# A Mamba block with butterfly FFN on one core: three moves in VectorE's order of work

## What is computed

```python
x = x + ssm(layernorm(x));  x = x + ffn(layernorm(x))
# ssm: xz = x @ in_proj_w.T; x_inner, z = split(xz)            (512 channels each)
#      x_conv = silu(causal_conv_4_taps(x_inner) + conv_b)
#      delta, B, C = split(x_conv @ x_proj_w.T), delta = softplus(delta)   (16 states)
#      h = h * exp(delta * A) + x_conv * (delta * B);  y = h . C           (scan over tokens)
#      return ((y + x_conv * D) * silu(z)) @ out_proj_w.T
# ffn: h = butterfly(x @ W_exp + b_exp); h = gelu(h + up_bias); h = butterfly(h)
#      return h @ W_con + b_con + down_bias
```

## Time and profile before

| | us |
|---|---|
| median of 3 runs | 543.41 (543.35 to 543.48) |
| the profiled execution | 543.8 |
| its span in the trace | 542.1 |
| PE busy in it | 516.0 (95%) |
| DVE busy in it | 416.8 (77%) |
| ACT busy in it | 307.0 (57%) |
| mean granted clock of PE | 0.981 of full |

### The profile page before, as it was taken

How to read it: one execution, slowest core, us unless ns; L and a number is a source line. 1 busy time by engine, 2 the same in 40 slices (tenths; PEclk the granted TensorE clock), 3 DMA queues, 4 the chain that set the end, 5 groups by cost and what they waited for, 6 DMA issues and landing times.

```text
span 542.1 us, 8227 instructions
## 1 busy us (share of the span) xinstructions
PE 516.0 (95%) x3012; PEld 422.5 (78%) x3012; DVE 416.8 (77%) x892; ACT 307.0 (57%) x537; POOL 93.3 (17%) x88
## 2 busy tenths in 40 slices
PE   4989999998999999999999999999999999889997
PEld 3756776776887788878888788888888789578886
DVE  4778999888984999489975999489956986576542
ACT  2777883794249622875269722964278514951242
POOL 4040200220211202140211211030213021122020
PEclk9995988999999999999999999999999999999999
DMA  9652511200112001210112002110021001200011
GB/s 223 134 28 3 83 39 41 66 16 2 39 40 76 6 2 50 69 41 1 40 40 81 0 2 79 54 28 2 0 79 42 1 1 39 81 0 1 1 40 39
DMA packets 42635, 21.75 MB, mean 40 GB/s; under 512 B 26435, under 2 KB 41027, under 8 KB 42596
## 3 DMA queue, kind: packets, MB, share of 16 engines
q1 hardware_dynamic: 39956, 17.57, 13.9%
q10 hardware_dynamic: 2640, 3.67, 2.4%
HBM read 16.78 MB, written 4.46 MB: 39 GB/s over the span
## 4 chain that ended last, share of the span: by engine, by line
PE 58%; DVE 20%; ACT 9%; issue 9%; POOL 2%; DMA 1%; DVEq 0%; ACTq 0%; POOLq 0%
PE wide L715 11%; PE acc L877 11%; PE wide L866 9%; PE wide L855 9%; DVE xc L1516 5%; PE wide L829 4%; DVE state L1621 3%; PE small L705 3%; PE wide L840 2%; ACT xc L1186 2%; DVE diag_sum L1639 2%; DVE diag L1635 2%; DVE hid_low L1533 1%; PE wide L725 1%; PE small L735 1%
## 5 line engine op out<-in xcount | busy, mean ns | idle before, releaser
L1146 ACT ACTIVATE hid_f<-wide,bias_up 128x512 f32<-128x512 f32 x64 | 43.9, 686 | 160.5 <-PE wide L866 157.5
L1516 DVE SCALAR_TENSOR_TENSOR xc<-xi,taps,xc 128x512 f32<-128x512 f32 x96 | 96.2, 1007 | 4.5 <-ACT xc L1177 2.3
L877 PE MATMUL acc<-w_down_high,hid_high 128*128 128x256 f32 x256 | 73.7, 288 | 3.5 <-DVE hid_low L1533 3.4
L877 PE MATMUL acc<-w_down_high,hid_low 128*128 128x256 f32 x256 | 72.0, 281 | 0.0
L877 PE MATMUL acc<-w_down_low,hid_high 128*128 128x256 f32 x256 | 72.0, 281 | 0.0
L1533 DVE TENSOR_TENSOR hid_low<-hid_f,hid_high 128x512 fp32r<-128x512 f32 x64 | 47.4, 743 | 15.5 <-ACT hid_high L1259 15.2
L855 PE MATMUL wide<-w_out,xc 128*128 128x256 f32 x256 | 58.4, 388 | 0.7 <-DVE xc L1660 0.5
L715 PE MATMUL wide<-xnT_ln1T_high,w_in_high 128*128 128x512 f32 x128 | 56.7, 443 | 0.0
L877 PEld LDWEIGHTS acc<-w_down_high,hid_high 128*128 128x128 f32 x256 | 48.3, 188 | 10.2 <-issue 6.6
L866 PE MATMUL wide<-xnT_ln2T_high,w_up_high 128*128 128x512 f32 x128 | 54.2, 424 | 1.7 <-DVE xnT_ln2T_low L1527 1.7
L855 PEld LDWEIGHTS wide<-w_out,xc 128*128 128x128 f32 x256 | 49.2, 194 | 7.8 <-issue 1.1
(11 more groups left out here) (193 smaller groups left out, 1035.3 us busy)
## 6 DMA issues: line engine op xcount, KB each, us to landing
x_res<-in_L_attn_x_dram SPq DMA_DIRECT2D x9, 512.0 KB, 3.5
c_near<-c_of_tokens SPq DMA_DIRECT2D x8, 512.0 KB
x_ln<-in_L_attn_x_dram SPq DMA_DIRECT2D x7, 512.0 KB, 3.6
out_dram<-x1b_xn SPq DMA_DIRECT2D x7, 512.0 KB, 2.9
xc<-in_L_attn_in_proj_w_dram ACTq DMA_DIRECT2D x2, 512.0 KB, 7.1
xc<-in_L_ffn_W_exp_dram ACTq DMA_DIRECT2D x1, 1024.0 KB, 11.1
x1b_xn<-in_L_ffn_W_con_dram ACTq DMA_DIRECT2D x1, 1024.0 KB, 15.0
raw_out<-n_L_attn_out_proj_w_dram ACTq DMA_DIRECT2D x1, 512.0 KB, 7.7
```

What stands on the lines that cost most here:

```text
L877: last = pe.matmul(acc[:, c, :], hid[h][:, j % HRING, c * P:(c + 1) * P], w_down[w][:, j, 0:DM], start=j == 0 and c % 2 == 0 and n == 0, s ...
L1146: ins = act.activation(out_ap, in_ap, how.pop("func"), **how)
L1516: ins = dve.scalar_tensor_tensor(xc[u % BATCH][:, e, :], xi[:, e, tap:tap + TILE], taps[:, e, tap:tap + 1], xc[u % BATCH][:, e, :], ALU.mu ...
```

## The change

Only VectorE's order of work is changed. Three things move:

1. The wait for `zeroed` leaves `constants()` and goes into `softplus`, for unit 0 only, in front of the first instruction that writes dA.
2. In phase 0 the statistics of unit 2 go from in front of gate 0 to behind gate 1, and its normalisation from between the gates to behind gate 3.
3. In phase 1 (the only one that uses `to_first_outputs`, since later phases take the form in halves) the convolution of channel block 0 of unit 2 goes from in front of `diagonal_times_c` to behind gate 3, and `low_hidden(p, 3)` now stands between the convolutions of blocks 0 and 1, so that it still has one convolution in front of it.

```diff
@@ constants()
                 link_setup(dve.tensor_tensor(rate_before[:, :, :], ...
-                dve.wait_ge(zeroed, 2)
@@ softplus(u)
                 dve.tensor_tensor(dB[:, :, :], ...).then_inc(dB_ready.handle, 1)
+                if u == 0:
+                    dve.wait_ge(zeroed, 2)
                 dve.tensor_tensor(dA[:, :, 0:NS], ...
@@ first_phase()
                 multiply_short_paths(DOWN)
-                first_stats(2)
                 gate(0, 0)
                 gate(0, 1)
-                first_normalise(2)
+                first_stats(2)
                 gate(0, 2)
                 gate(0, 3)
+                first_normalise(2)
                 multiply_whole_paths(DOWN)
@@ to_first_outputs(u, beside)
                 v, r, p = u + 1, u + 2, u - 1
-                convolve(v, 0)
                 diagonal_times_c(u)
@@
                 gate(u, 2)
                 gate(u, 3)
+                convolve(v, 0)
+                low_hidden(p, 3)
                 convolve(v, 1)
-                low_hidden(p, 3)
                 convolve(v, 2)
```

## The result

| | before | changed |
|---|---|---|
| median of 5 runs, us | 543.47 (543.35 to 544.11) | 546.75 (545.90 to 548.81) |
| ratio, 95% interval | 1 | 1.0069 (1.0042 to 1.0095) |
| profiled execution, us | 543.8 | 545.9 |
| its span, us | 542.1 | 543.8 |
| median span of the runs, us | 541.7 (26 later runs) | 544.7 |

The changed kernel is slower by 3.3 us in the median, near the forecast of 2.5 and inside its range. It also scatters: over 2.9 us, where the kernel before scatters over 0.8. The profiled execution is its fastest, only 2.1 above the one before; what is missing from it takes half of the experiments. One of the 27 later runs of the kernel before took 574.1 us, at a mean granted clock of 0.846, and is left out everywhere.

What follows compares the result with a forecast made beforehand. Each place was read by who arrives last: ScalarE's exponential in the start-up, TensorE after phase 0's gates, VectorE's unbroken list behind phase 1's. 0 + 0.3 + 2.24 = 2.5 on 543.41 gave 545.9 us, range 544.4 to 547.9.

Steps and rivals of the forecast that it cites:

- Start-up, 0 forecast: Start-up: normalisation starts earlier, but ScalarE's exponential at 34.79 stays, so moving the wait gains 0 us (at most 1.2).
- Gates, +0.3 forecast: End of phase 0: gates finish 1.3 earlier, but transposes hold the output projection back; +0.3 us, bounds 0 to +1.9.
- From there PE is the chain up to 119.36: From phase 0's output projection into phase 1: TensorE is the chain, so the projection's delay of 0.34 us passes on.
- w_down_low was forecast near 125.3: Sign in phase 1: VectorE's w_down_low comes near 125.3, against 124.99 in the kernel before.
- the rival of a full clock at that place: Phase 0's output projection: clock stays full, total +0.6 us, 544.0; chance 0.05.
- Convolution, +2.24 forecast: Phase 1: the convolution behind the gates delays VectorE's following work, and all 2.24 us reach TensorE's last 24 down products.
- w_down_low's idle at 2.66 as forecast (2.7): Phase 1: VectorE's wait for ScalarE's w_down_high before w_down_low grows from 0.42 to 2.7 us.
- the first wait: Behind phase 1's gates: TensorE first waits for hidden block 5, ready at 160.4 but wanted at 159.6.
- The paying start-up: Start-up: TensorE's step sums come earlier and VectorE's 1.18 us of idle goes; 544.7 us, chance 0.05.
- The hidden convolution: Phase 1: the moved convolution costs nothing, leaving only the gates' part; 543.8 us, no slowdown, chance 0.09.
- A low clock near 160: Phase 1: TensorE's new waits near 160 and 162 bring a low-clock stretch costing 1.9; 547.8 us, chance 0.08.
- The convolution at 4.24: Phase 1: the moved convolution costs 4.24 us, its time beside GpSimd's add; 547.9 us, chance 0.04.

Runs made afterwards that it cites:

- e1: Kernel before with only the wait for cleared buffers moved from constants() into softplus; 543.85 us, ratio 1.0008.
- e7: Kernel before with wait and gates moved, and TensorE's transposes of unit 2 put between the halves of phase 0's output projection; 544.03 us, ratio 1.0005.
- e3: Kernel before with only phase 1's convolution moved behind the gates; 545.65 us, ratio 1.0043.
- e8: Kernel before with hidden block 6's low part ahead of the second normalisation in all phases but the last; 543.82 us, ratio 1.0001.
- e9: Kernel before with a second convolution (channel block 1 of unit 2) put in front of the diagonal in phase 1; 545.96 us, ratio 1.0044.
- e10: Kernel before with phase 1's convolution moved, block 3's convolution behind the residual, low parts of blocks 5 to 7 ahead of the normalisation; 543.79 us, ratio 1.0000.
- e12: Kernel before with two thirds of convolve(v, 0) behind m_mat in phases 2 to 6, and block 6's low part ahead of the second normalisation; 548.41 us, ratio 1.0086.
- e6: Changed kernel with hidden block 6's low part ahead of the second normalisation in phase 1 only; 545.61 us, ratio to before 1.0042.
- e4: Kernel before with the wait and phase 0's gates moved, convolution left in its old place; 544.48 us, ratio 1.0018.
- e2: Kernel before with only phase 0's statistics and normalisation moved behind gates; 544.62 us, ratio 1.0020.

## Why the prediction was right, and where its sizes were off

The forecast of +2.5 came from one term that was right in size (2.24) and one that was too small for a reason that did not hold (0.3 for 0.8), and 0.4 us came from outside the span, where nothing was forecast. That 2.5 lies near the 3.3 and 2.9 measured rests on the convolution alone.

**Start-up, 0 forecast: right in the span.** The exponential stayed where it was, and e1's span is before's. The normalisation's 2.56 beside the memsets against 1.38 alone is what the cited rule on the lock between GpSimd and tensor_scalar (the Trainium skill, SBUF — State Buffer, Who interferes with whom) allowed for, and it ended before the transposes, as worked out; that the lock itself is the cause was not tested. Not foreseen: 0.3 to 0.4 us outside the recorded span in every kernel that has this part or the gates' part.

**Gates, +0.3 forecast: the delay right, its way to the end wrong.** The gates came earlier, y3's product lost its wait and the transposes held the projection back, as written; e7, which only takes them out of the way, brings the span back. The step that failed is "From there PE is the chain up to 119.36": the delay was taken to go through whole. In truth there was slack of 0.4 us behind the projection, so one execution pays 0, and another has more half-rate stretches on the transposes and the projection and pays 0.5 to 0.7 in the two traces taken, perhaps more in the longest runs, which no trace caught. In the median it is 0.8. One of the signs that were named shows it in the changed kernel's own trace: w_down_low was forecast near 125.3 and came at 124.51, which is 124.98 with the lead of 0.47, so of the 0.3 nothing had arrived. The forecast read one clock pattern as if it were the kernel's; the rival of a full clock at that place was real too, in the traces of e1, e3, e7, e8, e9, e10 and e12, and was worth nothing, because TensorE was not the bound.

**Convolution, +2.24 forecast: size right, route partly wrong.** 2.2 measured (e3), with w_down_low's idle at 2.66 as forecast (2.7). But the first wait was not for the low part of block 5. It came earlier, at up product 6, for the PSUM bank that the residual frees, with 1.59 of the 2.05; the rest was block 6. The prediction followed only VectorE's products and not the banks that it gives back. The size came out all the same, because everything in VectorE's unbroken list moved by the same 2.24 and TensorE had no slack at either place. Had the low parts been the only route, e6 would have mended the case; it took e10.

**The rivals.** The paying start-up is excluded by e1. The hidden convolution is excluded by e3. A low clock near 160 did not come: from 93 to 533 us the clock is full in all 14 traces. The convolution at 4.24 is excluded: one convolution behind the gates took 4.33 beside GpSimd's add, the others 2.3, before and after.

**Open.** The cause of the 0.4 us outside the span. And the longest spans of the changed kernel (546.5 to 546.7): the convolution's 543.9 (e3) and the most that e4's spans reach above before's median (543.8 against 541.7) make 546.0, so 0.5 to 0.7 are left over; none of these executions was caught in a trace. The profiled spans are accounted for: e2's and e4's (543.0 and 543.1) are 0.9 and 1.0 above that of before's profiled execution, of which the copy of the first state is 0.70 and 0.54 and the later end of VectorE's block 0.17 and 0.46.

## What to carry to other kernels

An instruction that stands in front of a wait is free up to the length of that wait, if nothing else needs what it delays; look at what follows the wait before moving it, since the place it goes to may have none. Along a full engine list ask what each instruction gives back (a bank, a buffer) as well as what it makes: the consumer of the space can be the first to wait. And if a kernel's time depends on where half-rate stretches fall, one trace shows one draw: compare the spread of the runs, and measure slack as the point from which a delay begins to count. Spans of two executions are comparable once they are cut at a row that both have: here the start-up alone wanders by 1.3 us, and what lies behind the cut agrees within 0.1 where the kernels are alike.

## What the runs showed of the hardware

The clock was at half in different places in different executions. Two traces of one program, the changed kernel, have it from about 87.3 to 90.7 and from about 86 to 89.4. Up to 118 us the kernel before, e8 and e10 are the same program too. Their traces show it near 74 to 77 and 87.5 to 91, near 75 to 78 only, and near 82 to 85.5 only. A first half-rate stretch, from 37 to 40 us on, was in every trace. Half-rate stretches cost nothing where TensorE was not the bound: 7.14 (e1) against 8.83 us (before) for the same 32 products left the time as it was.
